# Gathers of a half batch issued singly between GpSimd's norm factor and its three differences, in the projections of layer 1

## The reference, cut to what matters

```python
x = x + gb * _L0_ffn_ref(h, ...)                       # result of layer 0's experts, times a gate
h = _layernorm(x, axis=-1) * (1 + ca) + sa             # norm of layer 1
ct_q  = x @ Wd_q_w + Wd_q_b                            # in the attention, x is that h
qt    = heads(ct_q @ Wu_q_w + ...) + heads(_rope(ct_q @ Wq_r_w + ..., cos, sin))
ct_kv = x @ Wd_kv_w + Wd_kv_b
kt    = heads(ct_kv @ Wu_k_w + ...) + heads(_rope(x @ Wk_r_w + ..., cos, sin))
value = heads(ct_kv @ Wu_v_w + Wu_v_b)
```

## Time and profile before

| | |
|---|---|
| median of 3 runs | 1167.91 us (1163.81 to 1169.43) |
| profiled execution | 1166.31 us |
| its span, first to last instruction | 1164.2 us |
| busy: PE / DVE / ACT / POOL | 1044.9 / 948.4 / 780.3 / 329.8 us |
| mean granted TensorE clock | 0.959 of full speed |

### The profile page before, as it was taken

One profiled execution on the slowest core, in us unless ns is written; L12 is line 12 of the kernel. 1 busy time (PEld: TensorE's weight loads), 2 busy tenths in 40 slices (PEclk: granted clock), 3 DMA queues, 4 the chain that ended last, 5 costly groups with the idle time before them and its releaser, 6 DMA issues. The chain is left out here.

```text
span 1164.2 us, 23750 instructions
## 1 busy us (share of the span) xinstructions
PE 1044.9 (90%) x9028; PEld 493.3 (42%) x9028; DVE 948.4 (81%) x1442; ACT 780.3 (67%) x1559; POOL 329.8 (28%) x467
## 2 busy tenths in 40 slices
PE   6987699587678999999999999999999989889997
PEld 4786599443321222222222222222222229657655
DVE  7976555478889999999999999999999808966555
ACT  4543434144423999999999999999999984543421
POOL 4732367667520000000000000000000007347463
PEclk9998899898976999999999999999999999999999
DMA  7011276319980012220222101220120000423322
GB/s 242 1 37 37 87 202 203 107 34 213 202 222 1 8 30 35 35 35 3 35 35 36 28 10 35 35 34 17 22 35 3 2 3 3 158 79 98 93 62 81
DMA packets 94119, 76.81 MB, mean 66 GB/s; under 512 B 42900, under 2 KB 72980, under 8 KB 93496
## 3 DMA queue, kind: packets, MB, share of 16 engines
q1 hardware_dynamic: 89144, 65.33, 24.0%
q0 software_dynamic: 4864, 9.97, 3.4%
HBM read 47.74 MB, written 27.46 MB: 65 GB/s over the span
## 5 line engine op out<-in xcount | busy, mean ns | idle before, releaser
L1464 DVE TENSOR_REDUCE mx<-p_psA 128x1 f32<-128x1024 f32 x512 | 585.3, 1216 | 9.2 <-PE p_psA L1627 9.2
L1555 ACT ACTIVATE p_pt<-p_psS 128x512 f32<-128x512 f32 x1024 | 548.3, 597 | 37.7 <-PE p_psS L1649 18.0
L1662 PE MATMUL p_acc<-p_pt,V 128*32 128x256 f32 x4096 | 328.4, 392 | 15.4 <-ACT attn L1546 13.8
L1627 PE MATMUL p_psA<-K,Q 48*128 48x512 bf16 x1024 | 319.9, 395 | 9.4 <-DVE mx L1464 7.8
L1649 PE MATMUL p_psS<-Q,K 51*128 51x512 bf16 x1024 | 310.0, 384 | 0.0
L1662 PEld LDWEIGHTS p_acc<-p_pt,V 128*32 128x32 f32 x4096 | 82.0, 108 | 210.9 <-ACT p_pt L1555 110.4
L1381 POOL TENSOR_TENSOR mr<-zeros,mx 128x16 f32<-128x16 f32 x32 | 7.1, 221 | 546.9 <-DVE mx L1464 546.9
L1627 PEld LDWEIGHTS p_psA<-K,Q 48*128 48x128 bf16 x1024 | 57.1, 95 | 232.6 <-DVE mx L1464 197.7
L1649 PEld LDWEIGHTS p_psS<-Q,K 51*128 51x128 bf16 x1024 | 62.8, 93 | 18.1 <-ACT p_pt L1555 12.6
L1069 DVE TENSOR_TENSOR f_h<-f_bank,b 128x512 f32<-128x512 f32 x40 | 27.7, 692 | 38.2 <-PE f_bank L1137 38.2
L1029 ACT ACTIVATE f_h1T<-f_h 128x512 f32<-128x512 f32 x40 | 25.2, 629 | 31.5 <-DVE f_h L1069 31.5
(11 more groups left out here) (336 smaller groups left out, 1437.4 us busy)
## 6 DMA issues: line engine op xcount, KB each, us to landing
f_w<-in_w SPq DMA_DIRECT2D x40, 256.0 KB, 3.2
Q<-q_rows SPq DMA_DIRECT2D x32, 192.0 KB, 4.6
K<-k_rows SPq DMA_DIRECT2D x32, 192.0 KB, 5.1
hrows<-h SPq DMA_DIRECT2D x8, 512.0 KB, 3.2
result<-f_shared_kept SPq DMA_DIRECT2D x12, 256.0 KB
result<-f_y SPq DMA_DIRECT2D x10, 256.0 KB, 3.5
V<-v_rows SPq DMA_DIRECT2D x16, 144.0 KB, 5.6
x<-in_x SPq DMA_DIRECT2D x4, 512.0 KB, 5.6
```

The lines of the kernel that those rows point to most:

```text
L1464: dve.tensor_reduce(mx[v % 2][:, h, qt:qt + 1], psA[t][:], AX.X, ALU.max).then_inc(a_max, 1)
L1555: act.activation(pt[s % 2][:, head_at(s, j), :], psS[k % 3][:], ACT.Exp, scale=INV_SCALE).then_inc(s_out, 1)
L1627: mm = pe.matmul(psA[t][:, c * 512:(c + 1) * 512], Q[g % NBUF][rows, pair, q0:q0 + P], K[g % NBUF][rows, pair, c * 512:(c + 1) * 512], sta ...
L1662: mm = pe.matmul(acc[VW * h:VW * (h + 1), cols], V[g % NBUF][:, kc, h * (HD + 1):h * (HD + 1) + VW], pt[s % 2][:, h, cols], start=(kc == 0 ...
```

## The change

`gather` can now issue a part of its four DMAs, and the loop issues the four of half batch m + 4 one at a time: one after the norm factor of m + 2, one after the first difference of m, one after the second, one after the third. They were all behind the third. Half batches 4 to 7 are gathered this way; 0 to 3 as before. Nothing is added or removed, and the wait on `gathered[c - 1]` stays with the first of the four. The lines after L1333 move down by 2 to 5.

```diff
-                def gather(c):
-
-                    if c >= 1:
+                def gather(c, first=0, last=4):
+
+                    if c >= NM:
+                        return
+                    if c >= 1 and first == 0:
                         pool.wait_ge(gathered[c - 1], 64)
-                    for i in range(4 * c, 4 * c + 4):
+                    for i in range(4 * c + first, 4 * c + last):
...
                 def half(m):
...
+                    gather(m + 4, 0, 1)
                     pool.wait_ge(rest1[0], m + 1)
                     pool.wait_ge(part2[0], m + 1)
                     pool.tensor_tensor(parts[m // 2 % 2][2][:, 0, j], ...)
+                    gather(m + 4, 1, 2)
                     pool.wait_ge(full_ready[1], m + 1)
                     pool.wait_ge(part1[1], m + 1)
...
                     pool.tensor_tensor(rest[:, 1, :], ...)
+                    gather(m + 4, 2, 3)
                     pool.wait_ge(part2[1], m + 1)
                     pool.tensor_tensor(parts[m // 2 % 2][2][:, 1, j], ...)
...
                     half(m)
-                    if m + 4 < NM:
-                        gather(m + 4)
+                    gather(m + 4, 3, 4)
```

## The result

| | before | changed |
|---|---|---|
| median, 8 runs each | 1167.61 us | 1171.59 us (1170.71 to 1173.77) |
| ratio to before, 95% interval | | 1.0042 [1.0029, 1.0054] |
| profiled execution / its span | 1166.31 / 1164.2 us | 1170.71 / 1168.7 us |
| DVE busy / clock of TensorE | 948.4 us / 0.959 | 955.6 us / 0.953 |

The change made the kernel slower by 4.0 us of median, 0.34%; the ratio, 1.0042 with its interval, says 0.42%. All lines of the changed kernel are 2 to 5 higher than before: L1338 is the gather (L1336 before), L1346 the norm factor, L1355, L1361 and L1364 the three differences, L1401 the first instruction of combine, L1432 the addition in `whole`, L1423 the start of a rotation, L1468 the maxima.

What follows compares the result with a forecast made beforehand. DVE's going over to the maxima at 334.4 us was taken to bound the kernel. (c) + 4.1, (d) - 1.35 and (e) + 1.4 made + 4.2 us: predicted median 1172.1 us, 8-in-10 range 1165.0 to 1177.5.

Steps and rivals of the forecast that it cites:

- the likeliest case: Whole kernel: slower by + 2 to + 6 us, with + 4.2 us as the sum; chance 0.48.
- (a): GpSimd's norm factor, no longer behind four gathers, starts 1.37 us earlier where it was late, at half batches 3 and 5.
- (b): Two gathers now ahead of the second difference on GpSimd, 1.3 us each, take back up to 2.6 us.
- (c): GpSimd stands 5 us ahead of half batch 7's first gather until 6 has landed; key products late by 4.1 us.
- (e): TensorE idles ahead of a reduction, then reduction and key products may run at half clock: + 1.4 us, at most 3.5.
- (d): DVE's wait for the gathers of half batch 7 disappears: 1.35 us given back.
- port conflicts: Between GpSimd's differences and DVE: no direction seen, 0 us, with 1 us to both sides in the range.
- Short landings: Rival: lone gathers land in 2.5 to 4.9 us beside SP's traffic; faster by 2.4 us, 1165.5 us; chance 0.15.
- Waits in the slack: Rival: last gather of 6 lands by 292.5 and PE keeps its clock; + 0 to + 1 us, 1168.4; chance 0.19.
- The stall in full: Rival: last gather of 6 lands at 296.3, full clock loss, wait in (d) not returned; 1175.5 us; chance 0.18.

Runs made afterwards that it cites:

- second series: The changed kernel timed and profiled once more, on another chip, against the kernel before: ratio 1.0040, median 1174.25 us.
- run 9: Changed kernel without the `gathered[c - 1]` wait for half batches 4 to 7, plus an awaited memset between each gather and a following difference: 0.9970 of the kernel before.
- run 10: Changed kernel, one gather behind the second difference, three behind the third, no landing wait for 4 to 7, awaited memset before the third: 0.9987 of the kernel before.
- run 1: Changed kernel with the wait on `gathered[c - 1]` taken out for half batches 4 to 7: 1.0010 of the kernel before, 1169.23 us.
- run 5: Changed kernel with only the gathers of half batch 7 spread, those of 4 to 6 behind the third difference: 1.0055 of the kernel before, 1174.67 us.
- run 6: Changed kernel with only the gathers of half batches 4 to 6 spread, those of 7 behind the third difference: 0.9994 of the kernel before, 1167.69 us.
- Run 8: Changed kernel with 64 small unused products on TensorE ahead of the reduction of half batch 5: 1.0021 of the kernel before, 1170.78 us.
- run 7: Changed kernel with a small memset (the fence) behind each of the first three spread gathers, awaited by the next difference; landing wait kept: 1.0063 of the kernel before.
- run 4: Kernel before with all gathers of half batches 4 to 7 one half batch earlier, still in blocks of four: 1.0002 of the kernel before, 1168.52 us.

## Why the prediction was right, and where not

**The result.** Forecast + 4.2 us, measured + 4.0 of median (4.7 by the ratio of the second series); the likeliest case came in. That it fits to 0.2 us is luck: the first maximum was forecast at 338.6 and came at 340.29, 5.9 us later than before instead of 4.2, and the last stage, which the forecast does not treat, gave some 1.6 us back in this execution.

**(a) The norm factor.** The norm factors of half batches 3 and 5 start within 0.1 us of their variance (262.24 and 289.00), as forecast. Only the first is earlier than before (263.08); the second was at 288.11, since DVE's longer instructions make the variance late.

**(b) Two gathers ahead of the second difference.** By runs 9 and 10 no cost of them shows, though run 10 is no clean test of it. As a term it was inside (c).

**(c) The landing wait, the step on which the forecast stood.** Forecast 5 us of stall, 4.24 measured (3.81 in the second profile); last gather of 6 out at 284.2, measured 285.3; landing with 9.2 to 9.9, measured 9.1 to 9.4; second difference at 298.6, measured 298.31. Runs 1, 5 and 6 show it to be the cause: 3.5 us of 4.7 go with the wait, and the half batch with the longest landing alone costs as much as the whole. The number of stalls was missed: three or more and 6 to 12 us in all were forecast, two came, 1.34 and 4.24 us (2.46 and 3.81 in the second profile). The first gather of 6 found those of 5 landed.

**(e) The clock.** Forecast 1.4 of a possible 3.5 us: reduction and products took 2.07 and 1.59 instead of 1.12 and 1.02, 1.5 us. DVE took up the key products of 4 at 306.06, 5.3 us late; (c) and (e) together said 5.5. It stood only 1.17 us for them there, not 2 or more, and 1.05 us for ACT just before, since its own combine of 6 ended 2.9 us late. Run 8 brings 1.2 us of it back. A second stretch at the low level, at half batch 6 (the product at 325.68), was not forecast: DVE was 4.2 us late ahead of it, when it began the rest of half batch 5's queries (316.44 instead of 312.24), and 5.9 us behind it, at the key products (329.49 instead of 323.59).

**(d) Given back.** The wait for the gathers of 7 is gone, 1.35 us, as forecast: 312.18 has no idle time ahead.

**The step that failed: port conflicts, put at 0 with 1 us to both sides.** DVE's busy time grew by 7.1 us (run 7: all of it goes with the fence). That they cost something stood in the trace before, where an addition beside a difference took 1.64 us instead of 0.69, and ended 0.54 us behind it:

```profile
276.61 1.16 POOL L1352 TENSOR_TENSOR attn<-attn 128x512 bf16<-128x512 f32 x1
276.67 1.64 DVE L1428 TENSOR_TENSOR attn<-attn 128x512 f32<-128x512 f32 x1
```

I took the number of differences, which stays, for the cost, and not what stands ahead of them. That the sum came out all the same is because the stall would have held DVE back anyway: in run 7 the lock time turned into waiting, 23.5 us idle in the way against 12.4. With the landing wait taken out, the same lock is worth 4.7 us. So the forecast named a right cause and missed a cost of the same size that this cause hid.

**The rivals.** Short landings came in for the first gather of 6 only (2.7 us, out before SP's loads began). Beside these loads the others took 5.9, 9.1 and 9.4 us, and the wait goes by the last to land. The Trainium skill (DMA: Bandwidth & Descriptors, Queues, rings and completion order) has each DMA engine go round robin over its queues. That did not keep the gathers that went out alone at 282.7 and 285.3 short. Why they stay under way so long no run here tells. Waits in the slack came in for half batch 6, where GpSimd did not wait, not for 7. The stall in full needed the last gather at 296.3; it landed at about 294.7.

## What to carry to other kernels

A wait that costs nothing behind a long block of work can become the bound when the block is spread, though nobody touched it: for every wait on an engine's list, ask how long ago the awaited thing was issued, in the old order and in the new. Taking one cost away may show nothing while another covers it (run 7; run 4 took DVE's waits for gathers away and won nothing): test the candidates together as well as alone. And where one engine's instruction shuts out another's, as GpSimd's differences do DVE's additions here, count not only how often they meet but what is queued right ahead of it.

## What the runs showed of the hardware

A GpSimd difference of two 128x512 inputs that stands directly behind a gather shuts DVE's instructions with two inputs in SBUF out already while the gather runs. DVE's addition of 0.69 us took 2.23 at 254.13, from inside the gather (253.66 to 254.62) to 0.56 us behind the difference (254.64 to 255.80); those at 271.12 and 297.94 ended 0.56 and 0.55 us behind theirs. With a memset of 0.13 us in between, for which the difference waits, the same addition took its 0.69:

```profile
254.97 0.69 DVE L1438 TENSOR_TENSOR attn<-attn 128x512 f32<-128x512 f32 x1
```

though it ran beside this gather, in run 7:

```profile
254.68 0.97 POOL L1338 DMA_INDIRECT h<-result,slot  x1 [0.16 <-issue]
255.65 0.13 POOL L1360 MEMSET mr<- 128x16 f32 x1
255.85 1.16 POOL L1365 TENSOR_TENSOR attn<-attn,p_part 128x512 f32<-128x512 f32 x1
```

The Trainium skill (SBUF — State Buffer, SBUF: two separate sides) says that DVE and GpSimd share one port pair as an exclusive lock for a whole instruction, and that whichever starts first has it. The runs agree as to the lock, but by the recorded starts the first does not always have it: the addition began 0.51 us ahead of the difference, and still most of its work fell behind the difference's end. That DVE is shut out already during the gather is what these rows add. The profile's times on GpSimd are rough, so the fenced runs count for more here than one row.

A gather of 64 KB took 2.5 to 2.6 us from issue to landing in the quiet. With loads and stores on SP's queue it depended on when it went out: in a block from 283.1 to 287.1, with the loads under way since 277.5, 9.2 to 9.9 us for the first as for the last; issued alone, 2.7 us just before the loads began, 5.9 just behind their start, 9.1 and 9.4 later.
